# Cross-attention and quantised FFN on one core: scores and skip from fp16 halves, maxima scaled on VectorE, a new order of work

## The reference

```python
# _layernorm: (x - mean) / sqrt(var + 1e-5) over the last axis
def _L0_xattn_ref(pcd_up, pcd_down, Wq, Wk, Wv, Wskip):
    q = jnp.einsum('oc,bcn->bon', Wq, pcd_up)
    k = jnp.einsum('oc,bcm->bom', Wk, pcd_down)
    v = jnp.einsum('oc,bcm->bom', Wv, pcd_down)
    energy = jnp.einsum('bcn,bcm->bnm', q, k) / scale      # scale = sqrt(128)
    attention = jax.nn.softmax(energy, axis=-1)
    x = jnp.einsum('bnm,bcm->bcn', attention, v)
    skip = jnp.einsum('oc,bcn->bon', Wskip, pcd_up)
    return skip + x
def _L0_ffn_ref(x, qweight, scales, zeros, bias):
    w = _dequant_weight(qweight, scales, zeros)            # (w_int - round(zeros/scales)) * scales
    return jnp.einsum('bsi,io->bso', x, w) + bias
x = x + _L0_xattn_ref(_layernorm(x), ctx_1024, Wq, Wk, Wv, Wskip)
x = x + _L0_ffn_ref(_layernorm(x), qweight, scales, zeros, bias)
```

## Time and profile before

| | us |
|---|---|
| median of three runs | 528.22 |
| fastest, slowest of the three | 526.27, 528.64 |
| the profiled execution | 526.57 |
| its span | 524.6 |

### The profile page before, as it was taken

How to read it: one execution, slowest core, us unless ns; L and a number is a source line. 1 busy time by engine, 2 the same in 40 slices (tenths; PEclk the granted TensorE clock), 3 DMA queues, 4 the chain that set the end, 5 groups by cost and what they waited for, 6 DMA issues and landing times.

```text
span 524.6 us, 9213 instructions
## 1 busy us (share of the span) xinstructions
PE 496.9 (95%) x2668; PEld 302.8 (58%) x2668; DVE 427.5 (82%) x981; ACT 372.7 (71%) x844; POOL 470.8 (90%) x717
## 2 busy tenths in 40 slices
...
GB/s 300 191 69 137 161 196 185 190 194 179 178 184 194 167 187 193 192 171 185 204 163 186 182 195 174 192 202 160 184 182 201 174 179 209 159 134 138 147 142 102
DMA packets 227059, 92.65 MB, mean 177 GB/s; under 512 B 209472, under 2 KB 214080, under 8 KB 227008
## 3 DMA queue, kind: packets, MB, share of 16 engines
...
q10 hardware_dynamic: 720, 0.14, 0.1%
...
## 4 chain that ended last, share of the span: by engine, by line
PE 86%; POOL 7%; DVE 2%; DMA 2%; issue 1%; ACT 1%; POOLq 0%; SPq 0%
PE ps_y L924 41%; PE ps_e L889 15%; PE ps_o L919 14%; PE ps_o L915 8%; PE ps_kv L900 3%; PE ps_y L928 3%; PE ps_kv L902 2%; POOL sb_prob L255 2%; POOL sb_xc_lo L270 1%; DMA sb_xnt_lo<-sb_xn_lo 1%; DMA sb_x<-in_x_dram 1%; POOL sb_xn_lo L302 1%; ACT sb_prob L480 1%; DVE sb_st L596 0%; ACT sb_wf L512 0%
## 5 line engine op out<-in xcount | busy, mean ns | idle before, releaser
L924 PE MATMUL ps_y<-sb_wf,sb_xnt_hi 128*128 128x512 f16 x512 | 192.1, 380 | 4.4 <-DMA sb_xnt_lo<-sb_xn_lo 3.4
L924 PE MATMUL ps_y<-sb_wf,sb_xnt_lo 128*128 128x512 f16 x512 | 192.0, 379 | 0.0
L480 ACT ACTIVATE sb_prob<-ps_e,sb_neg_max 128x256 f32<-128x256 f32 x256 | 118.3, 470 | 57.2 <-DVE sb_neg_max L659 57.2
L255 POOL TENSOR_SCALAR sb_prob<-sb_prob,sb_rsum 128x256 f32<-128x256 f32 x256 | 122.7, 492 | 15.2 <-DVE sb_rsum L664 15.0
L668 DVE TENSOR_TENSOR sb_p_lo<-sb_prob,sb_p_hi 128x1024 f16<-128x1024 f32 x64 | 78.3, 1223 | 48.8 <-ACT sb_p_hi L489 48.8
L889 PE MATMUL ps_e<-sb_k_hi,sb_xc_hi 128*128 128x256 f32 x256 | 90.8, 355 | 10.4 <-DVE sb_k_lo L647 5.7
L249 POOL TENSOR_TENSOR sb_o<-sb_prod,sb_x 128x512 f32<-128x512 f32 x63 | 80.6, 1279 | 7.0 <-DVE sb_prod L702 7.0
L924 PEld LDWEIGHTS ps_y<-sb_wf,sb_xnt_hi 128*128 128x128 f16 x512 | 49.9, 98 | 63.8 <-DMA sb_xnt_lo<-sb_xn_lo 4.3
L659 DVE TENSOR_REDUCE sb_neg_max<-ps_e 128x2 f32<-128x512 f32 x128 | 84.8, 681 | 1.6 <-PE ps_e L889 1.2
L924 PEld LDWEIGHTS ps_y<-sb_wf,sb_xnt_lo 128*128 128x128 f16 x512 | 50.0, 98 | 56.7
L489 ACT ACTIVATE sb_p_hi<-sb_prob 128x1024 f16<-128x1024 f32 x64 | 67.4, 1053 | 19.8 <-issue 15.5
...
## 6 DMA issues: line engine op xcount, KB each, us to landing
...
sb_pt_hi<-sb_p_hi SPq DMA_TRANSPOSE x64, 3.0
sb_pt_lo<-sb_p_lo SPq DMA_TRANSPOSE x64, 2.8
...
sb_xnt_hi<-sb_xn_hi SPq DMA_TRANSPOSE x32, 2.8
```

The costliest lines, as they stand in the source:

```text
L255: last = pool.tensor_scalar(prob[:, j, t, :], prob[:, j, t, :], rsum[:, j, t:t + 1], P_SCALE, ALU.mult, ALU.mult)
L480: done = act.activation(prob[:, j, t, :], ps_e[j % 2][:, t, :], ACT.Exp, bias=neg_max[:, j, t:t + 1], accum_out=esum[:, j, t:t + 1])
L924: pe.matmul(ps_y[h][:, :], xnt_p[s][:, q % 2, kt, :], wf[:, kt, h * HALF:(h + 1) * HALF], start=kt == 0 and s == 0, stop=False)
```

## The change

The halves of scores and skip become fp16. So that they fit its range, `x` is now normalised before it is split (`centre` applies -mean/std and 1/std, scaled by 1024; `nb1` is a new DVE instruction, `negated_mean1`), and keys are scaled by the inverse of a bound, made by two one-column matmuls (`bound`) and three DVE instructions (`range_scales`). The scores come out scaled, so `row_max` is followed by an instruction that multiplies the two maxima by that scale (`neg_top`), and each exponential takes a scale from SBUF besides its bias. `nb2` moves from POOL to DVE (`negated_mean2`), the run-in's scaling of Wv and Wskip from DVE to POOL (`scale_weights`), and the orders of DVE, POOL and ACT change.

```diff
-        xc_hi, xc_lo = (sb(n, [P, 3, N], F32R) for n in ("xc_hi", "xc_lo"))
-        k_hi, k_lo = (sb(n, [P, 2, M], F32R) for n in ("k_hi", "k_lo"))
+        xc_hi, xc_lo = (sb(n, [P, 3, N], F16) for n in ("xc_hi", "xc_lo"))
+        k_hi, k_lo = (sb(n, [P, 2, M], F16) for n in ("k_hi", "k_lo"))
...
-        wsk_hi, wsk_lo = (sb(n, [C, 3, C], F32R) for n in ("wsk_hi", "wsk_lo"))
+        wsk_hi, wsk_lo = (sb(n, [C, 3, C], F16) for n in ("wsk_hi", "wsk_lo"))
...
+            def scale_weights():
+                pool.wait_ge(w_step, 5)
+                for w in (wv_sb, wskip_sb):
+                    pool.tensor_scalar(w[:, :], w[:, :], rw[:, :], None, ALU.mult).then_inc(w_scaled, 1)
...
-                last = pool.tensor_tensor(xc_lo[:, n % 3, cols], xc[:, cols], xc_hi[:, n % 3, cols].bitcast(F32),
-                                          ALU.subtract)
-                if h == HALVES - 1:
-                    last.then_inc(xclo_done, 1)
+                pool.tensor_tensor(xc_lo[:, n % 3, cols], xc[:, cols], xc_hi[:, n % 3, cols],
+                                   ALU.subtract).then_inc(xclo_done, 1)
             def inverse_std2(a):
                 pool.wait_ge(ve2_done, a + 1)
                 if ran(a, 1):
                     pool.wait_ge(xn_done, a)
                 pool.tensor_tensor(rstd2[:, :], ve2[:, :], neg_half[:, :], ALU.pow).then_inc(rstd2_done, 1)
-                pool.wait_ge(rstd2_done, a + 1)
-                pool.tensor_scalar(nb2[:, :], mv2[:, 0:1], rstd2[:, :], -1.0, ALU.mult,
-                                   ALU.mult).then_inc(nb2_done, 1)
...
                 if ran(b):
                     normalise(b, 1)
                     normalise(b, 2)
+                if ran(a):
+                    inverse_std2(a)
                 if ran(n):
                     centred_lo(n, 1)
-                if ran(a):
-                    inverse_std2(a)
                 if ran(b):
                     normalise(b, 3)
...
             def centre(n):
-                act.wait_ge(mv1_done, n + 1)
+                act.wait_ge(nb1_done, n + 1)
                 if ran(n, 1):
-                    act.wait_ge(xclo_done, n)
-                act.activation(xc[:, :], x_sb[:, n % 4, :], ACT.Identity, bias=mv1[:, 0:1],
-                               scale=-1.0).then_inc(xc_done, 1)
+                    act.wait_ge(xclo_done, HALVES * n)
+                act.activation(xc[:, :], x_sb[:, n % 4, :], ACT.Identity, bias=nb1[:, :],
+                               scale=rstd1[:, :]).then_inc(xc_done, 1)
...
             def exps(b, j):
                 act.wait_ge(max_done[j], b + 1)
                 if ran(b, 1):
                     act.wait_ge(plo_done[j // 2], b)
+                top = t_scale[:, b % 3, 1:2]
                 for t in range(TPC):
-                    done = act.activation(prob[:, j, t, :], ps_e[j % 2][:, t, :], ACT.Exp,
-                                          bias=neg_max[:, j, t:t + 1], accum_out=esum[:, j, t:t + 1])
+                    done = act.activation(prob[:, j, t, :], ps_e[j % 2][:, t, :], ACT.Exp, scale=top,
+                                          bias=neg_top[:, j, t:t + 1], accum_out=esum[:, j, t:t + 1])
...
             def run_in():
-                centre(0)
+                first_centre(0)
                 first_centred_hi(0)
                 keys_hi(0)
+                first_centre(1)
                 first_centred_hi(1)
                 keep_projections()
                 centre(1)
                 exps(0, 0)
                 exps(0, 1)
+                keys_hi(1)
                 centred_hi(1)
                 exps(0, 2)
                 probs_hi(0, 0)
                 exps(0, 3)
-                keys_hi(1)
                 values_hi(0)
+                exps(1, 0)
                 probs_hi(0, 1)
                 centre(2)
-                exps(1, 0)
+                exps(1, 1)
                 centred_hi(2)
-                exps(1, 1)
                 values_hi(1)
                 unpack(0)
...
+            def negated_mean1(m):
+                dve.wait_ge(rstd1_done, m + 1)
+                if ran(m, 1):
+                    dve.wait_ge(xc_done, m)
+                dve.tensor_scalar(nb1[:, :], mv1[:, 0:1], rstd1[:, :], -1.0, ALU.mult,
+                                  ALU.mult).then_inc(nb1_done, 1)
...
-            def value_scale(n):
-                dve.wait_ge(kv_done, n + 1)
-                dve.tensor_scalar(t_scale[:, :], ps_m[:, HALF - 1:HALF], TINY, 1.0 / V_TOP, ALU.max,
-                                  ALU.mult).then_inc(t_step, 1)
-                dve.wait_ge(t_step, 4 * n + 1)
-                dve.reciprocal(v_scale[:, :], t_scale[:, :]).then_inc(t_step, 1)
-                dve.tensor_scalar(o_scale[:, n % 3:n % 3 + 1], t_scale[:, :], w_inv[:, :], None,
-                                  ALU.mult).then_inc(t_step, 1)
-                dve.wait_ge(t_step, 4 * n + 3)
-                dve.wait_ge(rstd1_done, n + 1)
-                dve.tensor_scalar(sk_scale[:, :], v_scale[:, :], rstd1[:, n % 2:n % 2 + 1], P_SCALE, ALU.mult,
+            def range_scales(n):
+                dve.wait_ge(bound_done, n + 1)
+                if n == 0:
+                    dve.wait_ge(floors_made, 2)
+                    dve.wait_ge(w_step, 5)
+                t = t_scale[:, n % 3, :]
+                dve.tensor_tensor(t, (ps_o[0] if n == 0 else ps_m)[:, HALF - 2:HALF], floors[:, :],
+                                  ALU.max).then_inc(t_step, 1)
+                dve.wait_ge(t_step, 3 * n + 1)
+                dve.reciprocal(t_inv[:, n % 2, :], t).then_inc(t_step, 1)
+                dve.tensor_scalar(o_scale[:, n % 3:n % 3 + 1], t_scale[:, n % 3, 0:1], w_inv[:, :], None,
                                   ALU.mult).then_inc(t_step, 1)
...
             def values_lo(n):
                 dve.wait_ge(kvhi_done, n + 1)
-                dve.scalar_tensor_tensor(wsk_lo[:, n % 3, :], proj[:, SKIP, :], sk_scale[:, :],
-                                         wsk_hi[:, n % 3, :].bitcast(F32), ALU.mult, ALU.subtract)
-                dve.scalar_tensor_tensor(v_lo[:, n % 3, :], ps_kv[:, M:2 * M], v_scale[:, :],
+                dve.scalar_tensor_tensor(wsk_lo[:, n % 3, :], proj[:, SKIP, :], t_inv[:, n % 2, 0:1],
+                                         wsk_hi[:, n % 3, :], ALU.mult, ALU.subtract)
+                dve.scalar_tensor_tensor(v_lo[:, n % 3, :], ps_kv[:, M:2 * M], t_inv[:, n % 2, 0:1],
                                          v_hi[:, n % 3, :], ALU.mult, ALU.subtract).then_inc(kvlo_done, 1)
...
             def row_max(b, j):
                 dve.wait_ge(scores_done[j], b + 1)
                 dve.tensor_reduce(neg_max[:, j, :], ps_e[j % 2][:, :, :], AX.X, ALU.max,
-                                  negate=True).then_inc(max_done[j], 1)
+                                  negate=True).then_inc(top_done, 1)
+                dve.wait_ge(top_done, CHUNKS * b + j + 1)
+                dve.tensor_scalar(neg_top[:, j, :], neg_max[:, j, :], t_scale[:, b % 3, 1:2], None,
+                                  ALU.mult).then_inc(max_done[j], 1)
...
+            def negated_mean2(a):
+                dve.wait_ge(rstd2_done, a + 1)
+                if ran(a, 1):
+                    dve.wait_ge(xn_done, a)
+                dve.tensor_scalar(nb2[:, :], mv2[:, 0:1], rstd2[:, :], -1.0, ALU.mult,
+                                  ALU.mult).then_inc(nb2_done, 1)
...
                     stats2(a, 0)
                 if ran(b):
                     invert(b, 1)
+                if ran(m):
+                    negated_mean1(m)
+                if ran(a):
+                    residual(a, 1)
+                if ran(b):
+                    invert(b, 2)
+                if ran(a):
+                    stats2(a, 1)
+                    aggregate2(a)
+                if ran(b):
+                    row_max(b, 3)
                 if ran(n):
                     keys_lo(n)
+                if ran(a):
+                    negated_mean2(a)
+                if ran(n):
                     values_lo(n)
-                if ran(b):
-                    invert(b, 2)
-                if ran(a):
-                    residual(a, 1)
-                if ran(b):
-                    row_max(b, 3)
-                if ran(a):
-                    stats2(a, 1)
-                    aggregate2(a)
                 if ran(b):
                     invert(b, 3)
...
+            def bound(n, to):
+                pe.wait_ge(amax_done, n + 1)
+                peak = amax[:, n % 2:n % 2 + 1]
+                pe.matmul(to[:, HALF - 2:HALF - 1], top_inv[:, :], peak, start=True, stop=True)
+                pe.matmul(to[:, HALF - 1:HALF], kmax_row[:, :], peak, start=True, stop=True).then_inc(bound_done, 1)
...
             def scores(b, j):
+                if j == 0:
+                    pe.wait_ge(klo_done, b + 1)
+                if j % (CHUNKS // HALVES) == 0:
+                    pe.wait_ge(xclo_done, HALVES * b + 1 + j // (CHUNKS // HALVES))
```

(7 more changed lines are left out.)

151 lines of the change are left out of this document (81 added, 70 removed).

## The result

The changed kernel takes 587.63 us (median of four, 586.71 to 589.22) against 528.27 for the kernel before in the same runs: 1.114 times as long (95% interval 1.111 to 1.117). The forecast of 534 and its range were wrong; what happened is rival D, the neg_top that takes POOL's port, which had been given a chance of 0.16, at a price of 59 instead of 31 us.

What follows compares the result with a forecast made beforehand. The loop of DVE, ACT and POOL, at 15.4 us, was to replace PE's step of 15.22 as the bound: 526.57 + 28 x (15.4 - 15.22) + 2 for the run-in = 533.6, forecast 534 us, range 517 to 552.

Steps and rivals of the forecast that it cites:

- rival D: In DVE's loop, neg_top waits for POOL's port, 1.2 us a step: loop 16.1 to 16.6, time 559; chance 0.16.
- Four neg_top ... some 0.2 each: In DVE's loop, each neg_top behind its row maximum takes 0.196 plus a gap of 0.04.
- the sum: DVE's loop from the second product to the last reciprocal, terms added up: 10.33 us, before any hold.
- The exponentials' pointer costs nothing under cover: On ACT, the exponentials' second pointer, 0 to 0.19 an instruction, is hidden while wsk_lo is held.
- PE's step of 14.9: PE's own step falls to 14.9 us (14.85 to 15.2), with fp16 score matmuls at 0.109 each.
- The wait for nb2 goes, and normalisation and p_lo meet instead: Behind the last reciprocal, ACT's 1.49 wait goes; POOL's normalisation meets DVE's low half and takes 1.82.
- The gain of 0.5 behind the last reciprocal: From the last reciprocal to the next product, the loop takes 4.57 us instead of 5.1.
- The hold of wsk_lo, 0.5: On DVE, wsk_lo meets POOL's centred_lo and lengthens the loop by 0.4 to 0.6, taken as 0.5.
- The loop of 15.4 for A: Main case: the loop of DVE, ACT and POOL sets the step at 15.4 us; chance 0.38, 529 to 540.
- POOL "is not what is late": Among the covered edits: POOL loses 0.75 us a step and isn't what others wait for.
- Run-in +2: Before the steps, centre(1) waits for variance, power and nb1, behind a row maximum: +2 us, bounds 0 and 4.

Runs made afterwards that it cites:

- e1: The changed kernel with neg_top made by two one-column DVE instructions instead of one of two columns: 543.86 us, 1.031 of the kernel before.
- e8: The changed kernel with x normalised to one and keys unscaled, so no neg_top and no second pointer of the exponentials: 532.33 us, 1.009 of the kernel before.
- E3: The kernel before with only a neg_top added, one two-column instruction a chunk multiplying the maxima by a one: 578.89 us, 1.098 of the kernel before.
- e2: The changed kernel with neg_top made on ACT by a Copy with a scale, instead of on DVE: 543.55 us, 1.030 of the kernel before.
- e5: e1 with wsk_lo moved ahead of the last row maximum on DVE: 551.27 us, 1.046 of the kernel before.
- e11: e9 with the last chunk's normalisation moved from POOL to ACT and the probabilities' factor set to one: 523.89 us, 0.994 of the kernel before.
- e9: e8 with the step's old order of DVE and POOL, nb2 staying on DVE: 528.53 us, 1.002 of the kernel before.
- e6: e1 with the first low half of the probabilities moved behind the context maximum and product on DVE: 543.58 us, 1.031 of the kernel before.
- e10: e8 with the last chunk's normalisation moved from POOL to ACT and the probabilities' factor set to one: 531.83 us, 1.009 of the kernel before.

## Why the prediction was wrong, point by point

- *"Four neg_top ... some 0.2 each"* is the step that failed. The duration came from a one-column instruction; the two-column one takes 0.679. Four times 0.48 more is 1.9, as much as the 1.93 by which a step grew. Taken away alone, in e1, the hold gives back 17.15 - 15.66 = 1.5 of it, 44 of the 59 us; the rest of the scaling (neg_top's own time, the second pointer, the bound) is 11.5 more, from e1 to e8. E3 shows that it does this in the kernel before too, and e1, e2 that it is the form and the engine, not the wait for the maximum. The error lies in the first stretch of the loop alone: from the second product to the last reciprocal takes 334.85 - 322.28 = 12.57, where the sum had 10.33 and 0.5 for wsk_lo; from there to the next product takes 339.43 - 334.85 = 4.58, where it had 4.57.
- The row against rival D was misread. L591's 0.286 stood between the two paces: 127 more columns than L625's 0.196 took 0.09, where L721's pace (1024 elements in 0.68, of which one column has 0.15) would give 0.07 and half that pace 0.13. It was nearer to the faster one. The Trainium skill (Vector Engine (DVE) Microarchitecture Reference, 5.1) says that two elements from one SBUF source run in the mode that uses both ports. The trace agrees, with a pointer for the scalar too: 92 of 128 were held.
- D's own price was too low: it took an average POOL instruction, 0.66, at a random moment, 0.3 a time. Those that close the port are the subtractions, 1.16 long, and in this program they stand at fixed places: the last neg_top arrives just behind the start of centred_lo (332.44 against 332.40), because the variance ahead of the last maximum releases the power and then centred_lo. The mean of neg_top by chunk is 0.69, 0.25, 0.72 and 1.06.
- *The exponentials' pointer costs nothing under cover*: its size was within the bounds (0.559 against 0.470), and it was covered in e1; e5 shows it in the open.
- *PE's step of 14.9*: right. fp16 scores follow each other at 0.109, and e11's undisturbed steps, which have one one-column matmul less, are 14.83.
- *The wait for nb2 goes, and normalisation and p_lo meet instead*: right, 1.49 a step gone (8.1 is left in all, one wait in the tail) and 1.82 for the normalisation. The gain of 0.5 behind the last reciprocal is there in the trace, 4.58 against 5.11 before. But it doesn't pay for what the order costs ahead of it: e9 with the old order is faster than e8.
- *The hold of wsk_lo, 0.5*: hidden behind neg_top after the change; 0.50 - 0.34 = 0.2 in e1 (0.34 is its length in e5, where nothing holds it), 0.8 in e8. The loop of 15.4 for A was 15.66 in e1, which has one instruction a chunk more.
- *POOL "is not what is late"*: it has only 10% of the changed kernel's chain, but once neg_top is gone it holds 69% of e8's. A hold undone in one place comes back in the next (e6, e10). That the port is simply full is not shown, and e11 speaks against it: with the same work as e10 on both engines, two of three steps are PE's 14.83.
- *Run-in +2*: it was 6.4, above the upper end of 4. By the start of batch 3's scores (the row at 58.26 is of that batch, not of batch 2), neg_top's holds are 1.4 of it (62.90 in e1), the rest of the scaling 2.9 (60.04 in e8), and 2.1 remain, about what had been forecast for the wait for nb1; that they are that wait is not shown.

Left open: why the last residual of e10 always wins by those 0.05 us, what each edit of the run-in is worth by itself, and how the 11.5 us of the rest of the scaling divide: no run here takes away the exponentials' second pointer alone.
